# Third attention layer of an eight-layer program: how the parts of queries and keys are stored and loaded, the layout of the raw keys, and what is issued before the head loop

## The reference

```python
q, k, v = (qkv[0] * scale, qkv[1], qkv[2])
attn = jnp.einsum('bhid,bhjd->bhij', q, k)
qL = jnp.einsum('bhid,hdm->bhim', q, rpe_k_table)
attn = attn + jnp.take_along_axis(qL, idx, axis=-1)
kL = jnp.einsum('bhjd,hdm->bhjm', k * scale, rpe_q_table)
attn = attn + jnp.swapaxes(jnp.take_along_axis(kL, idx, axis=-1), 2, 3)
attn = jax.nn.softmax(attn, axis=-1)
out = jnp.einsum('bhij,bhjd->bhid', attn, v)
S = jax.vmap(lambda a, seg: jax.ops.segment_sum(a, seg, num_segments=NUM_BUCKETS))(a_t, rp)
out = out + jnp.einsum('inbh,hnd->bhid', S, rpe_v_table)
return x_out @ w_proj.T + b_proj
```

## Time and profile before

| | us |
|---|---|
| median of 3 runs | 2168.71 (2166.08 to 2169.61) |
| profiled execution, its own time | 2168.96 |
| its span in the trace | 2167.2 |
| DVE busy | 1644.3 (76%) |
| PE busy | 1763.1 (81%) |
| ACT busy | 1066.7 (49%) |
| POOL busy | 839.5 (39%) |

### The profile page before, as it was taken

How to read it: one execution, slowest core, us unless ns; L and a number is a source line. 1 busy time by engine, 2 the same in 40 slices (tenths; PEclk the granted TensorE clock), 3 DMA queues, 4 the chain that set the end, 5 groups by cost and what they waited for, 6 DMA issues and landing times. The chain is left out here.

```text
span 2167.2 us, 46455 instructions
## 1 busy us (share of the span) xinstructions
PE 1763.1 (81%) x16408; PEld 1296.3 (60%) x16408; DVE 1644.3 (76%) x3948; ACT 1066.7 (49%) x2023; POOL 839.5 (39%) x632
## 2 busy tenths in 40 slices
PE   6999974889888875599999568888877589996656
PEld 4777761555555652378888435565554378885434
DVE  6999996776777756789999857999999742225674
ACT  5888862555555421144555335666665233332632
POOL 3000006765555501134545345545554139802111
PEclk9999996999999996689999767999997779997877
DMA  4111102100000000000000185666665250000000
GB/s 122 56 56 47 47 16 76 35 19 19 18 19 19 19 1 5 13 13 26 25 25 12 18 255 149 160 175 168 154 160 129 54 207 20 19 0 7 1 1 23
DMA packets 133848, 129.45 MB, mean 60 GB/s; under 512 B 79797, under 2 KB 110363, under 8 KB 132914
## 3 DMA queue, kind: packets, MB, share of 16 engines
q1 hardware_dynamic: 132754, 126.80, 21.5%
q10 hardware_dynamic: 928, 0.47, 0.1%
HBM read 78.59 MB, written 40.81 MB: 55 GB/s over the span
## 5 line engine op out<-in xcount | busy, mean ns | idle before, releaser
L2848 ACT ACTIVATE l2a_pr<-l2a_ps_s,l2a_nm 128x512 f32<-128x512 f32 x256 | 174.3, 686 | 129.7 <-DVE l2a_nm L2771 129.5
L529 ACT ACTIVATE l0a_pr<-l0a_sm,l0a_nm 128x512 f32<-128x512 f32 x256 | 185.6, 726 | 43.7 <-DVE l0a_nm L398 42.3
L398 DVE CUSTOM_DVE_ANT_0 l0a_sm<-l0a_ps_s,l0a_tb 128x512 f32<-128x512 f32 x256 | 174.9, 684 | 21.6 <-PE l0a_ps_s L613 15.0
L2771 DVE TENSOR_REDUCE l2a_nm<-l2a_ps_s 128x2 f32<-128x1024 f32 x128 | 156.7, 1224 | 4.4
L2778 DVE STREAM_TRANSPOSE l2a_tt<-l2a_pr 128x1024 f32<-128x1024 f32 x128 | 157.9, 1234 | 0.6 <-ACT l2a_pr L2848 0.6
L621 PE MATMUL l0a_ps_p<-top_c_ident,l0a_pr 128*128 128x128 f32 x1024 | 155.5, 274 | 0.0
L1703 POOL TENSOR_TENSOR l1f_h<-l1f_lm,l1f_sg 128x512 f32<-128x512 f32 x72 | 93.0, 1291 | 152.0 <-DVE l1f_lm L1769 75.9
L621 PEld LDWEIGHTS l0a_ps_p<-top_c_ident,l0a_pr 128*128 128x128 f32 x1024 | 128.6, 141 | 22.0 <-issue 0.9
L2102 ACT ACTIVATE l2f_h<-l2f_ps_h 128x512 f32<-128x512 f32 x128 | 76.7, 600 | 132.1 <-PE l2f_ps_h L1615 126.1
L1831 ACT ACTIVATE l1f_csb<-l1f_ps_c,l1f_b3e 128x512 f32<-128x512 f32 x128 | 88.3, 690 | 102.8 <-PE l1f_ps_c L1615 94.0
L2069 DVE SCALAR_TENSOR_TENSOR l2f_acc<-l2f_ps_y,l2f_comb,l2f_acc 128x128 f32<-128x128 f32 x112 | 31.5, 344 | 133.6 <-PE l2f_ps_y L2143 133.6
(11 more groups left out here) (535 smaller groups left out, 5059.0 us busy)
## 6 DMA issues: line engine op xcount, KB each, us to landing
l_qband<-l2a_staged SPq DMA_DIRECT2D x16, 768.0 KB, 5.9
l2a_qb<-l_qband SPq DMA_DIRECT2D x64, 192.0 KB, 3.7
l2a_sb<-l_pband SPq DMA_DIRECT2D x128, 96.0 KB, 2.2
l0a_tb<-l_bias SPq DMA_DIRECT2D x16, 448.0 KB
l2a_ks<-l_k SPq DMA_DIRECT2D x16, 384.0 KB
l_pband<-l2a_pr SPq DMA_DIRECT2D x32, 192.0 KB, 3.4
l_pband<-l2a_pr SPq DMA_DIRECT2D x32, 144.0 KB, 2.0
l2f_upw<-in_L_ffn_up_weights SPq DMA_DIRECT2D x9, 512.0 KB, 11.6
```

The source lines that it names most:

```text
L398: v.tensor_tensor_reduce(sm[j % 4][:, :], ps_s[j % 2][:, :], tb[slot][:, off:off + N][:, ::-1], -1.0, 3e38, ALU.add, ALU.min, nm[:, j % 4: ...
L529: a.activation(pr[j % 4][:, :], sm[j % 4][:, :], ACT.Exp, bias=nm[:, j % 4:j % 4 + 1], scale=-1.0).then_inc(m["p_ready"], 1)
L2771: v.tensor_reduce(nm[:, g % 2, :], ps_s[g % 2][:, :, :], AX, ALU.max, negate=True).then_inc(m["nm_ready"], 1)
L2848: a.activation(pr[slot][:, 2 * (g % 2) + u, :], ps_s[g % 2][:, u, :], ACT.Exp, bias=nm[:, g % 2, u:u + 1], accum_out=rs[:, n % 2, 2 * (g % ...
```

## The change

- `q3`, `k3` get their three parts outermost and hold each part once. A batch's parts are stored by one DMA each for queries and the two versions of the keys, three a batch in place of nine. A head's 48 rows are loaded by `load_parts`, the helper of the first attention layer: three DMAs for the queries and three for the keys, of 24, 16 and 8 rows, which read a part as often as it is needed. So `HEAD_LOADS` is 7 in place of 3. The rows have the head's channel (8) outermost.
- `k32` is stored in whole rows of 512; the load of a head's raw keys reads 4 runs of 128 bytes for each partition, where it read one of 512 bytes.
- `parts` has four slots; ACT waits before batches 2 and 3 for the raw keys' store alone.
- ACT makes batch 0's bases before the last two copies of `zT`. DVE spreads the table after batch 2, not 0. POOL's fills stand in another order. SP zeroes the edges of the bands between the batches' stores, and loads the constant rows of `qs` and `ks` in the first block.
- Also in the first block, at its end: raw keys, shifts, parts and bias rows of head 0, the load of its band, and POOL's expansion of its keys. The store of `rv_d` stands behind that of the first band.

```diff
@@ l2_scratch
-    return {"q3": nc.dram_tensor("l2_q3", (P, len(Q_PARTS), T * P), BF16).ap(),
-            "k3": nc.dram_tensor("l2_k3", (P, len(K_PARTS), 2, T * P), BF16).ap(),
+    return {"q3": nc.dram_tensor("l2_q3", (3, P, T * P), BF16).ap(),
+            "k3": nc.dram_tensor("l2_k3", (3, P, 2 * T * P), BF16).ap(),
-            "k32": nc.dram_tensor("l2_k32", (P, HALF, B, N // HALF), F32).ap(),
+            "k32": nc.dram_tensor("l2_k32", (P, B, N), F32).ap(),
@@ l2_attn, helpers
-        HEAD_LOADS = 3
-        STORES = 1 + 3 + 2 * 3
+        HEAD_LOADS = 2 * len(PART_RUNS) + 1
+        ONCE_LOADS = 3
+        def load_raw_keys(sp, h):
+            each = N // HALF
+            src = bass.AP(k32.tensor, k32.offset + h * HD * T * P, [[each, HALF], [T * P, HD], [N, B], [1, each]])
+            sp.dma_start(rawk[h % 2][:, :].rearrange("p (b g) -> p b g", b=B), src).then_inc(keys_loaded[h % 2], 16)
@@ first block
-            parts = p.sb("parts", [P, 2, 3, 3, N], BF16)
+            parts = p.sb("parts", [P, B, 3, 3, N], BF16)
@@ first block, SP
                 for b in range(B):
                     cols = slice(b * N, (b + 1) * N)
                     sp.wait_ge(m["base_ready"], 4 * b + 4)
-                    sp.dma_start(k32[:, :, b, :], base[:, b % 2, 2, :].rearrange("p (c g) -> p c g", c=HALF)).then_inc(stored[b % 2], 16)
+                    sp.dma_start(k32[:, b, :], base[:, b % 2, 2, :]).then_inc(k32_stored[b % 2], 16)
+                    blank(b)
                     sp.wait_ge(m["q_lo"], b + 1)
-                    for first, count, part in Q_ROW_RUNS:
-                        sp.dma_start(q3[:, first:first + count, cols], parts[:, b % 2, 0, part:part + 1, :].broadcast_to([P, count, N])).then_inc(stored[b % 2], 16)
+                    sp.dma_start(q3.rearrange("c p t -> p c t")[:, :, cols], parts[:, b, 0, :, :]).then_inc(m["q3_stored"], 16)
                     for v in range(2):
                         sp.wait_ge(m["lo_ready"], 2 * b + v + 1)
-                        for first, count in K_ROW_RUNS:
-                            sp.dma_start(k3[:, first:first + count, v, cols], parts[:, b % 2, v + 1, 0:count, :]).then_inc(stored[b % 2], 16)
+                        sp.dma_start(k3.rearrange("c p t -> p c t")[:, :, v * T * P + b * N:v * T * P + (b + 1) * N],
+                                     parts[:, b, v + 1, :, :]).then_inc(m["k3_stored"], 16)
+                for i in range(2):
+                    sp.wait_ge(k32_stored[i], 16 * (B // 2))
+                sp.wait_ge(m["tab_stored"], 16)
+                load_raw_keys(sp, 0)
+                load_shifts(sp, 0)
                 sp.wait_ge(m["g_lo"], 1)
...
+                sp.wait_ge(m["q3_stored"], 16 * B)
+                load_parts(sp, qs[0], q3, 0, head_loaded[0], True)
+                sp.wait_ge(m["k3_stored"], 16 * 2 * B)
+                load_parts(sp, ks[0][:, :, :].rearrange("p v t -> p (v t)"), k3, 0, head_loaded[0], False)
                 sp.wait_ge(m["g_stored"], 16 * B)
+                load_bias_rows(sp, 0)
                 sp.wait_ge(m["zeroed"], 16 * (QBAND_RING + 2 * PBAND_RING))
                 sp.wait_ge(m["l_ready"], ROUND["q", 0, 3])
                 sp.dma_start(qband[0][:, 0:ROW], staged[0][:, :, :].rearrange("p a n -> p (a n)")).then_inc(q_stored[0], 16)
+                sp.wait_ge(m["rvd_ready"], B)
+                sp.dma_start(rv_d.rearrange("h p n -> p h n"), rvd[:, :, :, :].rearrange("p h k n -> p h (k n)")).then_inc(m["rvd_stored"], 16)
+                sp.wait_ge(q_stored[0], 16)
+                for b in range(B):
+                    sp.dma_start(qb[0][b * GRP:(b + 1) * GRP, :, :].rearrange("p a n -> p (a n)"), skewed(qband[0], b, GRP - 1, -1, ROW)).then_inc(qband_read[0], 16)
+                sp.wait_ge(m["rvd_stored"], 16)
@@ first block, ACT
-                        a.wait_ge(stored[b % 2], 16 * STORES * (b // 2))
+                        a.wait_ge(k32_stored[b % 2], 16 * (b // 2))
@@ second block, SP, head_scores
-                    sp.dma_start(q[0:KROWS, :], q3[h * HD:(h + 1) * HD].rearrange("d c t -> (d c) t")).then_inc(sem, 16)
-                    sp.dma_start(k[0:KROWS, :, :].rearrange("p v t -> p (v t)"),
-                                 k3[h * HD:(h + 1) * HD].rearrange("d c v t -> (d c) (v t)")).then_inc(sem, 16)
+                    load_parts(sp, qs[h % 2], q3, h, head_loaded[h % 2], True)
+                    load_parts(sp, ks[h % 2][:, :, :].rearrange("p v t -> p (v t)"), k3, h, head_loaded[h % 2], False)
+                    load_bias_rows(sp, h)
```

More of the change, by code:

```diff
@@ L2271, in l2_attn @@
         xk = s.sb("xk", [P, GRP + T * P + GRP + HALF])
+        qs = [s.sb(f"qs{i}", [L2_ROWS, T * P], BF16) for i in range(2)]
+        ks = [s.sb(f"ks{i}", [L2_ROWS, 2, T * P], BF16) for i in range(2)]
+        rawk = [s.sb(f"rawk{i}", [P, T * P // HALF]) for i in range(2)]
+        kshift = [s.sb(f"kshift{i}", [P, WINDOW_COLS]) for i in range(2)]
+        qb = [s.sb("qb0", [P, NB, BAND])]
         ps_s = [s.ps(f"ps_s{i}", [P, 2, N]) for i in range(2)]
@@ L2374, in _ @@
                 g.memset(zero_rows[:, :], 0.0).then_inc(m["pad_ready"], 1)
+                ln.powers(g, 1)
+                g.memset(ones3[:, :], 1.0).then_inc(m["ones_ready"], 1)
+                ln.powers(g, B, start=1)
                 g.memset(rvd[:, :, :, :], 0.0).then_inc(m["zero_ready"], 1)
-                ln.powers(g, B)
-                g.memset(ones3[:, :], 1.0).then_inc(m["ones_ready"], 1)
                 g.memset(xk[:, 0:GRP], 0.0).then_inc(m["once_ready"], 1)
@@ L2459, in _, with copy_z, bases @@
                 a.copy(wT[:, :, :], ps_x.rearrange("p (i d) -> p i d", d=D)).then_inc(m["wT_ready"], 1)
[L2460 removed]
+                last = R_N - 1
+                by_block = lambda x: x.rearrange("p (k j) -> p k j", j=GRP)
+                def copy_z(b):
                     a.wait_ge(m["t_ready"], b + 1)
[L2462 to L2465 removed]
+                    a.copy(zT[:, :, b, :], by_block(ps_t[b % 2])).then_inc(m["zT_ready"], 1)
+                def bases(b):
                     a.wait_ge(m["qk_ps"], 2 * b + 2)
                     if b >= 2:
[L2468 removed]
+                        a.wait_ge(k32_stored[b % 2], 16 * (b // 2))
                         a.wait_ge(m["res_ready"], 3 * (b - 1))
                         a.wait_ge(m["gam_ps"], b - 1)
[L2471 removed]
                     a.activation(q32[:, :, b, :], by_block(ps_q(b, 0)), ACT.Copy, scale=SCALE).then_inc(m["base_ready"], 1)
@@ L2479, in _ @@
                         if i == 0:
-                            a.copy(by_block(parts[:, b % 2, 0, 0, :]), q32[:, :, b, :]).then_inc(m["hi_ready"], 1)
+                            a.copy(by_block(parts[:, b, 0, 0, :]), q32[:, :, b, :]).then_inc(m["hi_ready"], 1)
                         else:
-                            a.copy(parts[:, b % 2, i, 0, :], base[:, b % 2, i - 1, :]).then_inc(m["hi_ready"], 1)
+                            a.copy(parts[:, b, i, 0, :], base[:, b % 2, i - 1, :]).then_inc(m["hi_ready"], 1)
+                copy_z(0)
+                copy_z(1)
+                a.wait_ge(m["t_loaded"], 32)
+                bases(0)
+                copy_z(2)
+                copy_z(3)
+                highs(0)
+                for b in range(1, B):
+                    bases(b)
+                    highs(b)
                 a.wait_ge(m["gam_ps"], B)
@@ L2749, in _ @@
                     if i == 7 and h + 2 < HEADS:
-                        expand(h + 2)
+                        expand(g, h + 2)
                 ln.powers(g, 2 * B, start=B)
```

126 lines of the change are left out of this document (52 added, 74 removed).

## The result

The changed kernel takes 2171.11 us (median of 20 runs, 2168.45 to 2176.57) against 2168.54 (20 runs) for the kernel before on the same chip: ratio 1.0013, with a 95% interval of 1.0007 to 1.0019. That is 2.6 us slower where 3.0 us faster was predicted, and just above the range's end of 2171. It lies within 0.2% of no change.

A forecast was written before the change was run, and what follows sets the result against it. DVE was taken to bound the head loop, so gain could come only before its first row there: the second block opening at 1284.5 instead of 1287.47, 3.0 us earlier, all else zero, gave 2168.71 - 3.0 = 2165.7 us, range 2159 to 2171.

The forecast's parts named there:

- the last key part is ready 5.9 later, at 1268.3: First block: DVE begins batch 3 at 1262.4, so POOL finishes the last key part at 1268.3, 6.4 us earlier.
- fit between its powers: First block: POOL's fills fit between its powers and, with constant rows and zeroing, cost zero.
- the two engines' splits: First block, split of batches: if the two engines' splits slow each other, the gain is 1.5 us less.
- I take 4.6: End of first block: landing of the first band's store, taken as 4.6 us between 3.4 and 5.9.
- the store of `rv_d` ... is through by then: End of first block: the store of rv_d lands within at most 4.7 us, so it does not delay the opening.
- SP's sum: First block: SP's issues from the last key part to the band's store sum to 9.4 us, store at 1277.7.
- the gain isn't there: Rival: split bound by POOL or stores still crowding; opening at 1287, time 2168.5; a part of the forecast's 0.58 chance.
- ACT's stop would go: First block: ACT no longer stops before batch 2, where it stood 7.59 us.
- 20.7 us from opening to DVE's first row: Second block: the chain from PE's opening to DVE's first loop row stays at 20.7 us despite the early loads.
- The rival of late raw keys: Head loop: raw keys landing beyond 6.5 us delay each of 14 heads; 2172.7 at 7 us, 2180 at 7.5; chance 0.12.
- a DMA as releaser of POOL's expansion in the loop: Head loop: sign of a wrong prediction, POOL's expansion being released by a DMA; no size given.
- The rival that it rises later: Start of head loop: PE's clock rises a step later, costing up to 3 us; time 2168.7; chance 0.08.

The follow-up runs named there:

- tabq_first: Changed kernel with POOL's band table made ahead of batch 0 instead of batch 2; ratio 1.0009 to the kernel before.
- layout_only: Kernel before with only the storage changed: parts stored once and read in three loads, raw keys in whole rows; ratio 0.9987 to the kernel before.
- both_first: Changed kernel with both the spreading copies and POOL's band table moved before batch 0; ratio 1.0010 to the kernel before.
- early_and_first: Changed kernel with spreading before batch 0, and the first band's read and the wait for rv_d's store in the second block; 2159.57 us, ratio 0.9962.
- before_filled: Kernel before with PE's idle stretches in the first block filled by matmuls nobody reads; ratio 1.0009 to the kernel before.
- loads_late: Changed kernel with head 0's loads, band read and expansion back in the second block, rv_d stored and awaited before the band's store; ratio 0.9987 to the kernel before.
- spread_first: Changed kernel with the four spreading copies moved from behind batch 2 to before batch 0; ratio 1.0007 to the kernel before.
- best_raw: best with the band table back in batch 2 and head 0's raw keys, shifts and expansion in the first block; 2161.0 us, ratio 0.9967 to the kernel before.
- raw_filled: best_raw with PE's idle stretches in the first block filled by matmuls nobody reads; 2160.95 us, ratio 0.9969 to the kernel before.
- open_early: Changed kernel with the first band's read and the wait for rv_d's store moved to the second block; ratio 0.9992 to the kernel before.
- rvd_only: Changed kernel with only the wait for rv_d's store moved to the second block; ratio 1.0016 to the kernel before.
- best: loads_late with spreading and band table before batch 0 and the wait for rv_d's store in the second block; 2157.91 us, ratio 0.9950 to the kernel before.

## Where the prediction was right and wrong

**The step that failed first: "the last key part is ready 5.9 later, at 1268.3".** It was 1273.4, 5.1 us late. Its own terms, against the rows after: batch 0's split ended at 1249.1 and not 1248.0. Ahead of it a small row of the normalization took 1.64 us where its like take 0.17; it ended with a fill of POOL's beside it, which the prediction had put at zero ("fit between its powers"). No run took the fill away. Batches 1 and 2 took 13.9 us and not 9.4 (5.7 and 8.2, from one copy of the values to the next). The spreading and the last 5.9 us were as said. I took the 4.72 us between two copies from the kernel before, where ACT's wait kept POOL and DVE apart, and gave the slowing of "the two engines' splits" 1.5 us as a bound. The second cause I missed altogether: POOL's band table. It stood in the same place of POOL's list before, and the trace of before already shows its price, 2.38 us for a row that takes 0.69. There it cost nothing, because ahead of batch 3 DVE had to wait 1.73 us for ACT in any case:

```profile
1259.67 2.75 POOL L2383 TENSOR_TENSOR l2a_tabq<-l2p_ext,top_c_headmask 128x1536 f32<-128x1536 f32 x1
```

```profile
1260.59 2.38 DVE L2421 TENSOR_TENSOR l2p_res<-l2a_q,l2p_parts 128x512 f32<-128x512 f32 x1 [1.98 <-ACT l2p_parts L2480]
```

With ACT ahead nothing hid it. tabq_first shows 2.4 us of this. The Trainium skill, "SBUF — State Buffer", section on its two sides, says that a DVE operation with two SBUF inputs and a POOL operation that reads SBUF exclude each other for a whole instruction. The trace agrees: the DVE row of 3.24 us began after POOL's of 3.20 and ended 0.55 us behind it, as the one of 2.38 did in the kernel before, and without POOL such a row is 0.68. Asking of each POOL operation which DVE rows it would now meet would have found it.

**The second: "I take 4.6" for the band's landing, and "the store of `rv_d` ... is through by then".** The band's store was issued at 1282.56 and SP issued the reads at 1288.63, 6.1 us later, near the median of the earlier trace rows (5.9), which was the upper end of my term. `rv_d`, issued 0.4 us behind it, landed after some 8.4 us and not within 4.7; that it could be last had no price. From the band's store to the opening it took 9.3 us where 6.8 were predicted, 2.5 too many: some 1.5 in the landing and 1.1 in the wait for `rv_d`. I had named `rv_d` as a load on the queues and priced it too low: the landings of 3.4 to 3.5 us, one of which was the lower end of my term, are all of kernels that had waited for that store first.

These are all: 5.1 and 2.5, less 0.25 as SP's sum was 9.15 us and not 9.4, are 7.35, which is the 3.0 promised and 4.4 lost (1291.87 against 1287.47).

**The rival "the gain isn't there"** had part of the mechanism, a split held up by POOL, but only to an opening of 1287, because I let the landing's terms reach no further. No case had both at their ends. An interval for the opening of 0.2 to 6.2 us of gain was too narrow: the block's new tail, 9.3 us, had never been seen in a trace and deserved its worst case.

**Right:** that ACT's stop would go, SP's pauseless list, the six loads by three for 1.97 and 1.86 us (I had 2.13), 20.7 us from opening to DVE's first row, and the loop: it took 402.8 us to the end (404.0). The rival of late raw keys did not come true. One of the signs set for a wrong prediction did, a DMA as releaser of POOL's expansion in the loop (6.3 us in nine waits), but it cost nothing: PE has no wait for the expansion in 1345:1725. The row behind the figure of 0.42 that the prediction gives for a single load is the first one below, of the kernel before; the others are of the changed kernel:

```profile
1418.34 0.42 SPq L2596 DMA_DIRECT2D l2a_ks<-l_k  x1
```

```profile
1421.84 1.94 SPq L182 DMA_DIRECT2D l2a_qs<-l_q  x3
1423.82 1.86 SPq L182 DMA_DIRECT2D l2a_ks<-l_k  x3
...
1426.49 0.59 SPq L2309 DMA_DIRECT2D l2a_rawk<-l_k  x1
```

Counted from the first load of the bundle, raw keys were issued 4.7 us later (1421.84 to 1426.49), against 1.7 before (1417.88 to 1419.58): 2.9 us more, where the prediction had 3.4. They landed in at most 4.6 us, well under its limit of 6.5, so runs of 128 bytes did not make them late.

**The clock.** The rival that it rises later was given 0.08. Its rises, counted from DVE's first row and read from windows of 4 us: 10 to 12 us after it in before, after, layout_only, both_first, early_and_first and before_filled, 16 to 17 in loads_late, tabq_first, spread_first, best_raw and raw_filled, 29 in open_early, 32 in rvd_only. In `best` it rose ahead of the loop, fell, and rose again after 11. Where it took over 15, DVE's third step to its fourth lasted 5.4 us instead of 3.7 to 4.1, and to the end it took 404.9 to 407.6 us; elsewhere 402.8 to 404.9. rvd_only, in which PE was busy throughout and yet at half clock for 12 us on end:

```profile
1328.00:1332.00 4.00, 4.00 (x34) 0.50 0.72 248
1332.00:1336.00 4.00, 4.00 (x37) 0.50 0.47 98
1336.00:1340.00 4.00, 4.00 (x35) 0.50 0.30 82
```

(Columns here: window, us, PE busy, PEclk, DMA share, GB/s.) The Trainium skill, "TensorE: Matmul & The Clock Gate", section on the HAM clock gate, says that the point of the rise varies for one and the same kernel. The 10 to 32 us here are of 14 kernels with one profile each, so they neither bear that out nor speak against it. These 2 to 5 us are seen and not explained. The gains follow the openings all the same, a microsecond for a microsecond to within 3 us; whether the clock is what the rest hangs on is not shown.

## What to carry to other kernels

When a wait goes that kept two engines apart, re-time every operation that will now stand side by side, those the edit doesn't touch included, and not only the ones it moves. A transfer that starts at the very end of a block and must land inside it is paid in full: keep at the end of a block only what the next needs at once, and move the waits for the rest to their first reader. Take a change apart before judging it; here its layout was worth 2 to 3 us, its tail cost 8 of the opening and some 5 of the time, and with two small repairs the whole was worth 7.6.

## What the runs showed that I had not expected

- A DVE row of 0.68 us with two SBUF inputs took 3.24 beside one POOL operation of 3.20, and DVE's spreading copies 5.29 beside another in place of 2.67 alone.
- A single SP issue of a load took 4.61 us where its like take 0.6, in early_and_first, 0.8 us after the store of `rv_d` and 1.2 after the band's, with the 16 DMA engines busy (share 1.02 in 1283:1288). In open_early, with the same order there, it took 4.65. The opening did not wait for it.

```profile
1282.46 0.42 SPq L2414 DMA_DIRECT2D l_rv<-l2a_rvd  x1
1283.28 4.61 SPq L2310 DMA_DIRECT2D l2a_rawk<-l_k  x1
```

- Loads in runs of 128 bytes landed no later than those of 512: 3.2/4.0/4.6 us against 2.9/4.8/5.8.
- A band's store of 768 KB landed in 3.4 to 3.5 us when SP had waited for the store of `rv_d`, of the same size, and in 4.6 to 6.1 when that was issued within 2.1 us of it.
- TensorE's clock went to half speed within 2.5 us of idleness at the block's border, though PE had been kept busy until then, and stayed at half speed through 12 us in which PE was busy all the time.
